# A differential-attention layer in which the FFN of one token tile is laid beside the attention of the next, with its weights streamed from HBM

## The reference

```python
s1 = einsum('bhqd,bhkd->bhqk', q1, k1) * scale      # q1, k1, q2, k2 = x @ Wq1, ...
s2 = einsum('bhqd,bhkd->bhqk', q2, k2) * scale
a1 = softmax(where(causal, s1, -inf)); a2 = softmax(where(causal, s2, -inf))
lam = exp(sum(lq1 * lk1)) - exp(sum(lq2 * lk2)) + LAM_INIT      # one number per head
out = einsum('bhqk,bhkv->bhqv', a1 - lam * a2, v)               # v has 32 dimensions
normed = (out - mean(out)) * rsqrt(var(out) + eps)              # over the 32
x = layernorm(x + merge(normed * (1 - LAM_INIT)) @ Wo)
```

```python
h = silu((x @ w1.T) * s1) * ((x @ w2.T) * s2)
h = gelu((h @ h1.T) * hs1);  h = gelu((h @ h2.T) * hs2)
x = layernorm(x + (h @ w3.T) * s3)
```

## Time and profile before

| | us |
|---|---|
| median of 3 runs | 2097.22 (2093.45 to 2098.77) |
| profiled execution | 2093.8 |
| its span | 2091.4 |
| PE busy in the span | 1925.5 |
| ACT busy | 1468.2 |
| DVE busy | 724.6 |
| POOL busy | 201.2 |

### The profile page before, as it was taken

How to read it: one execution, slowest core, us unless ns; L and a number is a source line. 1 busy time by engine, 2 the same in 40 slices (tenths; PEclk the granted TensorE clock), 3 DMA queues, 4 the chain that set the end, 5 groups by cost and what they waited for, 6 DMA issues and landing times. The chain is left out here.

```text
span 2091.4 us, 36204 instructions
## 1 busy us (share of the span) xinstructions
PE 1925.5 (92%) x12400; PEld 1090.7 (52%) x12400; DVE 724.6 (35%) x1543; ACT 1468.2 (70%) x1876; POOL 201.2 (10%) x300
## 2 busy tenths in 40 slices
PE   7994599999899899998999999399999999999997
PEld 5883233333233233332333333278888888888886
DVE  5775021222122221221122212344554535445442
ACT  5663499989899899898998999254444435445452
POOL 0001111111111111111111111000000000000000
PEclk9997699999999999999999999699999999999998
DMA  8997805643366235642564340200101000110000
GB/s 264 361 354 200 134 6 78 83 62 55 51 82 83 36 51 81 83 56 32 79 82 57 52 57 11 81 1 31 31 11 31 22 22 21 33 31 11 11 11 12
DMA packets 137064, 148.83 MB, mean 71 GB/s; under 512 B 76000, under 2 KB 108256, under 8 KB 133760
## 3 DMA queue, kind: packets, MB, share of 16 engines
q1 hardware_dynamic: 134768, 140.55, 33.8%
q10 hardware_dynamic: 1888, 5.24, 1.3%
q0 software_dynamic: 240, 0.66, 0.2%
HBM read 90.85 MB, written 55.57 MB: 70 GB/s over the span
## 5 line engine op out<-in xcount | busy, mean ns | idle before, releaser
L811 ACT ACTIVATE attn_probs<-attn_s_ps 128x1024 f32<-128x1024 f32 (+2 forms) x1152 | 1013.5, 1049 | 112.8 <-PE attn_s_ps L830 106.6
L850 PE MATMUL attn_sums_ps<-attn_probs,heads_v 128*32 128x512 f32 (+3 forms) x5120 | 611.9, 551 | 0.0
L830 PE MATMUL attn_s_ps<-heads_q,heads_k 50*128 50x512 f32 (+3 forms) x2560 | 475.0, 435 | 93.4 <-DMA heads_q<-shift 48.5
L830 PEld LDWEIGHTS attn_s_ps<-heads_q,heads_k 50*128 50x128 f32 x2560 | 218.1, 188 | 577.3 <-ACT attn_probs L811 465.8
L1334 ACT ACTIVATE split_whole<-split_hid_ps,hs 128x512 f32<-128x512 f32 x128 | 88.3, 690 | 274.5 <-PE split_hid_ps L1248 274.3
L895 DVE COPY attn_sums_sb<-attn_sums_ps 128x512 f32<-128x512 f32 x64 | 44.3, 692 | 670.4 <-PE attn_sums_ps L850 666.8
L795 POOL TENSOR_SCALAR_AFFINE_SELECT attn_probs<-attn_probs 128x512 f32<-128x512 f32 x256 | 161.2, 639 | 955.8 <-ACT attn_probs L811 954.6
L1248 PE MATMUL split_hid_ps<-split_hid_b,h2t_r 128*128 128x512 f32 x1024 | 240.6, 392 | 0.0
L1248 PE MATMUL split_hid_ps<-split_hid_a,h1t_r 128*128 128x512 f32 x1024 | 238.1, 391 | 0.0
L1248 PEld LDWEIGHTS split_hid_ps<-split_hid_a,h1t_r 128*128 128x128 f32 x1024 | 190.0, 188 | 41.2 <-DVE split_hid_a L1476 1.4
L1248 PEld LDWEIGHTS split_hid_ps<-split_hid_b,h2t_r 128*128 128x128 f32 x1024 | 189.8, 188 | 38.0
(11 more groups left out here) (123 smaller groups left out, 1567.2 us busy)
## 6 DMA issues: line engine op xcount, KB each, us to landing
qk_parts<-proj_parts SPq DMA_DIRECT2D x64, 512.0 KB, 5.6
heads_q<-qk_parts SPq DMA_DIRECT2D x90, 256.0 KB
heads_k<-qk_parts SPq DMA_DIRECT2D x90, 256.0 KB
proj_w_rows<-in_L_ffn_h_w SPq DMA_DIRECT2D x16, 512.0 KB, 6.5
values<-proj_v SPq DMA_DIRECT2D x8, 1024.0 KB, 6.0
diffs<-attn_diff SPq DMA_DIRECT2D x32, 256.0 KB, 4.5
split_heads<-diffs SPq DMA_DIRECT2D x8, 1024.0 KB, 5.5
heads_v<-values SPq DMA_DIRECT2D x15, 512.0 KB
```

The lines of the kernel that those rows point to most:

```text
L811: nc.scalar.activation(weights, side_by_side, ACT.Exp, scale=SCALE).then_inc(exp_done, 1)
L830: last = nc.tensor.matmul(s_ps[n % SLOTS][:, s, place * width:(place + 1) * width], k_sb[u][rows, b * SEQ + j * PARTS:b * SEQ + (j + 1) * ...
L850: last = nc.tensor.matmul(sums[c * D:(c + 1) * D, off:TILE], v_sb[u][:, b * KEY_BLOCKS + j, :], probs[k % PROBS][:, b, s, off:TILE], start ...
```

## The change

The attention phase and the FFN are merged into one `fused_phase`, and nothing in it is a loop any more: all 128 pairs of stage and head are written out. A stage is one query tile t (0 to 3, of 512 queries) of one batch; for each of its 16 heads PE goes over the 4t + 4 key blocks. The order of all engines comes from a `Plan`, which numbers units (one exponential each: 4t + 3 per head, 1152 in all), and gives each piece of other work the number of the unit after which it is issued. On PE each unit issues its scores, then, two quads later, the sums of a quad, then the transposes of a finished head, then as many FFN pieces as are due. A quad is two key blocks of one batch with both softmaxes, again four results side by side; the two halves are added on DVE before the transpose (`fold`), which is now made per head and stage. The FFN of a stage's 512 tokens is laid over the units of the stage after the next boundary, spread by the cost of its pieces, with its last product one stage later; the FFN of the last stage stands alone at the end.

Keys, queries and values are loaded per head and stage (15 DMAs each, of `(t + 1) * 512` keys), into room for eight key tiles. The FFN weights are laid out on the host in the order of use; the projection phase only copies them within HBM, and the fused phase streams them in 20 chunks of 512 KB per stage through a ring of three. w3 and Wo stay. The check for `wide` is made on those chunks in the fused phase. x comes transposed from the host too, so that both kinds of transposes leave the projection phase, with the rounding and comparing of the weights. Attention's results stay on chip for the FFN (they are also stored, for the fp32 way). SiLU is made with Tanh, the square roots by steps on DVE, GELU on pairs of blocks, four blocks at a time. There are two score buffers instead of three, and two banks for the FFN instead of eight. The loads of the first head, and the memsets of ones, have moved behind `maximum_phase`. The diff, cut to its core:

```diff
-        ffn_w = (w1, w2, h1, h2, w3)
-        finish = ctx.enter_context(Room(nc, "finish"))
-        with ExitStack() as weights:
-            rounded = {name: weights.enter_context(nc.sbuf_tensor(f"{name}_r", shape, F32R)) for name, shape in FFN_SHAPES}
-            project_phase(nc, keep, rounded, x, (wq1, wq2, wk1, wk2), wv, (lq1, lk1, lq2, lk2),
-                          ffn_w, (s1, s2, hs1, hs2, s3), qk_parts, values)
-            with Room(nc, "heads") as room:
-                heads = head_buffers(room)
-                maximum_phase(nc, keep, heads, qk_parts, shift, values)
-                attention_phase(nc, keep, heads, qk_parts, shift, values, diffs)
-            sems = finish_sems(nc, finish)
-            finish_phase(nc, keep, sems, "split", True, rounded, x, wo, diffs, out)
-        whole_w = {name: sb(f"{name}_f", shape) for name, shape in FFN_SHAPES}
-        turn_weights_phase(nc, keep, ffn_w, whole_w)
-        finish_phase(nc, keep, sems, "full", False, whole_w, x, wo, diffs, out)
+        sems = finish_sems(nc, ctx.enter_context(Room(nc, "finish")))
+        project_phase(nc, keep, x_t, (wq1, wq2, wk1, wk2), wv, (lq1, lk1, lq2, lk2), (s1, s2, hs1, hs2, s3), ffn_t, ffn_r, qk_parts, values)
+        maximum_phase(nc, keep, qk_parts, shift)
+        fused_phase(nc, keep, x, wo, ffn_r, qk_parts, shift, values, diffs, out)
+        whole = sb("ffn_f", [PARTS, WEIGHT_COLS])
+        load_weights_phase(nc, keep, ffn_t, whole)
+        finish_phase(nc, keep, sems, whole, x, wo, diffs, out)
...
-                        sp.wait_ge(x_turned, EC * t + EC)
+                        sp.wait_ge(xt_low, EC * t + EC)
                         load_x(t + 2, u)
-                    if 1 <= m <= 4:
-                        if m == 1:
-                            sp.wait_ge(w_turned, 1 + WG * t)
-                            sp.wait_ge(compared, 2 + UNITS * t)
-                        if more:
-                            load_w(t + 1, 1 - u, m - 1)
-                        elif m == 1:
-                            sp.dma_start(w_rows[1 - u][:, 0:EC * HIDDEN].rearrange("p (o i) -> p o i", o=EC), w3.rearrange("(o p) i -> p o i", p=PARTS)).then_inc(w3_loaded, 16)
+                    if m == 1:
+                        sp.dma_start(ffn_r[:, bass.ts(t, SHARE)], ffn_t[:, bass.ts(t, SHARE)]).then_inc(weights_copied, 16)
...
+                    if c == 0:
+                        act.wait_ge(x_loaded[u], 16 * r + 16)
+                    nc.scalar.copy(xt[u][0][:, c, :], x_sb[u][:, c, :]).then_inc(xt_high, 1)
...
+LAG = 2
+SLOTS = 2
+PROBS = 8
+LOAD_SLOTS = 4
+KEY_TILES = 8
+HEAD_DELAY = 12
+NORM_DELAY = 8
+BREAK = 6
+GROUP = 4
+RAW = 6
+RING = 3
+FLAG_TILE = 6
+ROOT_OPS = 11
+STAGES = [(t, b) for t in range(QUERY_TILES) for b in range(BATCH)]
+STEPS = [(i, h) for i in range(len(STAGES)) for h in range(HEADS)]
+LOADS = STACK_DMAS + 1 + 2
...
+def step_quads(t):
+    full = [[[(2 * n, 0, TILE, 0)], [(2 * n + 1, 0, TILE, 0)]] for n in range(SUBS * t // 2)]
+    d = SUBS * t
+    second = PARTS if t else 0
+    first_two = [[(d, 0, TILE, 0)], [(d + 1, second, TILE - second, 0)]]
+    last_two = [[(d + 2, 2 * PARTS, 2 * PARTS, 0), (d + 3, 3 * PARTS, PARTS, 2 * PARTS)]]
+    if t == 0:
+        return [first_two, last_two]
+    return full[:t] + [first_two] + full[t:2 * t - 1] + [last_two] + full[2 * t - 1:]
...
+        self.weigh_at = [quad_unit(q + LAG) for q in range(self.nq)]
+        self.fold_at = [quad_unit(q + LAG) for q in self.last_quad]
+        self.turn_at = [quad_unit(q + LAG + 1) for q in self.last_quad]
+        self.square_at = [n + 2 for n in self.turn_at]
+        self.sum_at = [n + 4 for n in self.turn_at]
...
+            total = sum(cost for _, cost, _ in pieces)
+            end = begin + total if tail else self.stage_unit[i + 2]
+            pace = total / (end - begin - (0 if tail else BREAK))
+            done, now = 0.0, begin
+            for label, cost, delay in pieces:
+                now = max(now, begin + delay, begin + done / pace)
...
+                for s in range(2):
+                    for n in range(len(QUERY_PLACES)):
+                        rows = slice(s * HALF_ROWS + n * HEAD_DIM, s * HALF_ROWS + (n + 1) * HEAD_DIM)
+                        sp.dma_start(k_sb[rows, k_cols].bitcast(F32),
+                                     qk_parts[1, KEY_PLACES[n], h * HEAD_DIM:(h + 1) * HEAD_DIM, s, b * SEQ:b * SEQ + keys]).then_inc(loaded[slot], 16)
+                        sp.dma_start(q_sb[rows, slot, :].bitcast(F32),
+                                     qk_parts[0, QUERY_PLACES[n], h * HEAD_DIM:(h + 1) * HEAD_DIM, s,
+                                              b * SEQ + t * TILE:b * SEQ + (t + 1) * TILE]).then_inc(loaded[slot], 16)
+                    row = s * HALF_ROWS + SCORE_ROWS
+                    sp.dma_start(q_sb[row:row + SHIFT_ROWS, slot, :].bitcast(F32),
+                                 shift[:, h, s, b * SEQ + t * TILE:b * SEQ + (t + 1) * TILE]).then_inc(loaded[slot], 16)
+                sp.dma_start(v_sb[:, plan.place[g] * SUBS:(plan.place[g] + t + 1) * SUBS, :],
+                             values[h, :, b * KEY_BLOCKS:b * KEY_BLOCKS + (t + 1) * SUBS, :]).then_inc(loaded[slot], 16)
...
+                        nc.scalar.activation(tanh[:, m % 2, :], ffn_ps[plan.use["up", i, m, 0] % 2][:, :], ACT.Tanh, scale=half_s1[:, m:m + 1]).then_inc(tanh_done, 1)
+                    for layer in range(2):
+                        for m in range(0, HC, 2):
+                            yield plan.gelu_at(i, layer, m)
+                            slot = (cuts(i, layer + 1, m) - 1) % RAW
+                            act.wait_ge(emptied, plan.use["hid", i, layer, m + 1] + 1)
+                            nc.scalar.activation(raw[:, slot:slot + 2, :], raw[:, slot:slot + 2, :], ACT.Gelu).then_inc(gelu_done, 1)
...
+            def scores(n):
+                g, pieces, _ = plan.units[n]
+                i = STEPS[g][0]
+                slot = g % LOAD_SLOTS
+                if n == plan.first_unit[g]:
+                    pe.wait_ge(loaded[slot], 16 * LOADS * (g // LOAD_SLOTS) + 16 * LOADS)
+                if n >= SLOTS:
+                    pe.wait_ge(exp_done, n - SLOTS + 1)
+                for j, off, cols, place in pieces:
+                    key = plan.place[g] * TILE + j * PARTS
                     for s in range(2):
                         rows = slice(s * HALF_ROWS, s * HALF_ROWS + STACK_ROWS)
-                        last = nc.tensor.matmul(s_ps[n % SLOTS][:, s, place * width:(place + 1) * width],
-                                                k_sb[u][rows, b * SEQ + j * PARTS:b * SEQ + (j + 1) * PARTS],
-                                                q_sb[u][rows, b * SEQ + t * TILE + off:b * SEQ + (t + 1) * TILE], start=True, stop=True)
+                        last = nc.tensor.matmul(s_ps[n % SLOTS][:, s, place:place + cols], k_sb[rows, key:key + PARTS], q_sb[rows, slot, off:off + cols],
+                                                start=True, stop=True)
                 last.then_inc(scored, 1)
 
-            def weigh(h, u, k):
-                t, j = STEPS[k]
-                off = window(t, j)
-                sums = sums_ps[t % 2]
-                pe.wait_ge(exp_done, NU * h + LAST_UNIT[k] + 1)
-                if j >= SUBS * t:
-                    pe.wait_ge(masked, SUBS * NT * h + MASKS[k])
-                if j == 0:
-                    pe.wait_ge(sums_bank_free, NT * h + t + 1)
-                for b in range(BATCH):
-                    for s in range(2):
-                        c = 2 * b + s
-                        last = nc.tensor.matmul(sums[c * D:(c + 1) * D, off:TILE], v_sb[u][:, b * KEY_BLOCKS + j, :], probs[k % PROBS][:, b, s, off:TILE],
-                                                start=(j == 0), stop=(k == END[t]))
-                last.then_inc(probs_free, 1)
-            def turn(h, t):
-                pe.wait_ge(sums_copied, NT * h + t + 1)
-                for i in range(SUBS):
-                    last = nc.tensor.transpose(sums_ps[t % 2][:, i * PARTS:(i + 1) * PARTS], sums_sb[:, i * PARTS:(i + 1) * PARTS], keep["ident"][:, :])
+            def weigh(q):
+                g, units, is_first, is_last = plan.quads[q]
+                sums = sums_ps[g % 2]
+                pe.wait_ge(exp_done, units[-1] + 1)
+                if plan.masks[units[-1]] > (plan.masks[units[0] - 1] if units[0] else 0):
+                    pe.wait_ge(masked, plan.masks[units[-1]])
+                if is_first and g >= 2:
+                    pe.wait_ge(sums_free, g - 1)
+                for n in units:
+                    for j, off, cols, place in plan.units[n][1]:
+                        group = j % 2 if len(plan.units[n][1]) == 1 else 1 - j % 2
+                        for s in range(2):
+                            c = 2 * group + s
+                            last = nc.tensor.matmul(sums[c * D:(c + 1) * D, off:off + cols], v_sb[:, plan.place[g] * SUBS + j, :],
```

(21 more changed lines are left out.)

1147 lines of the change are left out of this document (688 added, 459 removed).

## The result

The changed kernel takes **2803.7 us** (median of 4 runs, 2793.5 to 2805.4) against 2095.3 before: a ratio of **1.337** (95% interval 1.333 to 1.341). The forecast was 2398 with a range to 2550. The direction was right, the loss was forecast at 303 us and is 708.

The account below looks back on a forecast made before the run. TensorE was taken as the bound, with 9% of slack: first scores 210, stage 0 101, stage 1 136 + 39, later stages 1724, GELU breaks 62, tail 124 make 2396, plus 2.4 around it: 2398 us, range 2110 to 2550.

Parts of the forecast that it names:

- The fixed cost of each change of kind: On PE in the fused stages: 0.22 us into scores, 0.14 into sums, 0.15 into transposes, 0.20 into FFN pieces.
- The turn that no row had shown: From a row-tiled score pair to the full array on PE: drains too; without a drain some 80 us lower.
- Rival (a): Turns on PE are free, weight loads being fetched while score matmuls stream: 272 us go, 2126; chance 0.10.
- (b): PE's idle time is filled: free turns, FFN pieces cover GELU's breaks, loads issued at 0.31 us: 2034; chance 0.11.
- The first scores: Start of attention after projections, fill, memsets and first loads: at 210 us against 232.04 before; bounds 190 and 232.
- SP's issues: 15 DMAs per head's step at 6.3 us; SP bounds stage 0, which takes 101 us.
- GELU between exponentials: Breaks on ScalarE of 4.5 us or so, 4 per stage; PE reaches the third unit 2.6 us early: 62 us.
- rival (d): Only the table switches on ScalarE cost more, with a 1.38 us drain each: 2464; chance 0.08.
- VectorE, POOL, streaming of weights. Covered by PE.: In the fused stages VectorE needs 140 us per stage, of PE's 218 at t = 1, so no cost was added.
- Loads per step: Head loads cost SP 6.3 us per step; hidden from stage 2 on, where a step lasts over 13 us.
- Rival (c): Loads late at t = 2 and 3: each of the 64 steps waits 3 us, 2590; chance 0.11.

## Why the prediction was wrong

**Right, and the larger part of the mechanism.** The fixed cost of each change of kind, worked out from the earlier trace rows: turns and columns of the six long stages come to 1720 us by the new trace's counts (1237 of columns, 483 of turns) for the forecast 1724, and the split leaves 1709 us of work at full clock. With 352 blocks and 395 changes away that work fell by 127 us for 157 (the 30 between them stay open), and with 433 blocks away and 37 changes more by 79 for 79. The turn that no row had shown costs as much as the others: from the start of a score pair to that of an FFN piece is 0.43 us, as to a sum group, where a second pair follows after 0.23. The Trainium skill, "TensorEngine Tiling (Array Packing)", section Key Properties, says that a change of the tiling mode drains TensorE; the traces agree. Rival (a) is out, and (b) with it. The first scores (212 for 210) were right too, and SP's issues nearly: 7.0 us per step in stage 0 for 6.3, which over 15 steps is the 11 us by which that stage is too long.

**The step that failed is what stands in those stages beside columns and turns.** They last 2116 us. That leaves 396 for TensorE's waits and its half clock, where the forecast had one term, 62 us of GELU breaks. In the trace 232 of them are idle time, and most of the rest is the half clock: TensorE works 352 us at 1.2 GHz in these stages. Three parts of it:
- *"GELU between exponentials", 62 us, mis-sized*: 157 measured. The wait was near what I took: TensorE stands 73 us at the 24 breaks of the six stages (stage 1 has four more, which the term left out). I left out that nearly every break is followed by 3 to 17 us at 1.2 GHz, in a forecast whose columns all ran at full clock. The earlier trace rows showed 0.98 for attention, and I took that for a property of attention, not of work without gaps. The Trainium skill, "ScalarE: Activation LUTs" (What ACT_TABLE_LOAD costs), gives a switch 1.28 us of load and 1.38 us of drain, which is rival (d), 2464. The load agrees (1.28 us here); the drain shows on no row of ScalarE, where the load begins 0.03 us after the exponential, and two switches with a small GELU take 2.8 us in the kernel before. The measurement decides. That 157 us lie near 149, a load and a drain for each of 56 switches, is luck: the breaks last as long as their rows say, and the rest is TensorE's clock.
- *"VectorE, POOL, streaming of weights. Covered by PE."* failed. I compared sums, 140 us of VectorE with 218 of TensorE, and a sum says nothing of a chain of 48 instructions that stands in front of a fold: 73 us with its half clock. Some 18 of them are the two waits behind y's store again, and 11 lie in the tail.
- *"Loads per step ... from stage 2 on a step lasts over 13 us and hides it"* held for the issues. What was missed is a DMA in front of them that waits: 44 us. The prediction had asked for each queue that a step is moved past, and it looked at what SP issues, not at what SP waits for.

With these three removed, and the turns and SP's issues shortened, the six stages last 1752 us, of which 1561 are columns and the turns left. So 396 has become 191: **the three carry up to 205 us in these stages** (some 20 of them came with the shortened turns alone), less than their single prices since the waits partly overlap. Of the 191, 113 are idle time, and at most 47 half clock. They are short waits in the fixed order of five engines, for the exponential just before, for a bank of the two that the FFN has, for the heads' scaling ahead of the output projection; none was tested by itself, and that part stays argued. So do the 29 us in stage 1 and the 33 in the tail, where TensorE's clock was 0.82 and 0.87, but for the 11 of the tail that the normalizations' chains took.

Rival (c), late loads at t = 2 and 3, was right in kind and wrong in cause: two waits of 20 us, not one of 3 in each step. The range failed for the same reason as the rivals: each was one wait at its own price, none said that waits also lower the clock, and none was all of them at once.

## What to carry over

Beside an engine with 9% of slack, nothing that it must do is free: count the changes of matmul kind and price each from a narrow timeline, 0.14 to 0.22 us here, before the columns. In an order written out by hand for five engines, look for each queue at the longest chain or wait that it now holds in front of short work; a comparison of busy sums will not show it. And forecast waits with the clock behind them: 67 us of waits at the breaks put into the kernel before cost 62 more at half clock, and with the table loads gone from the changed kernel 58 us of idle time went in the six stages and up to 104 of half clock.
